# Expert slots in two phases and a router in batches of 4, 8 and 4 tiles, on one core of a Trainium2

## The chip, the cores and the metric

One core of one Trainium2 chip runs the whole program. The metric is the device time of one execution in microseconds (us), the median of three runs. Its engines work in parallel, each through its own queue in order: TensorE (PE; its weight loads are shown as PEld), VectorE (DVE), ScalarE (ACT), GpSimd (POOL) and SyncE (SP), which only starts transfers. Semaphores tie them together.

## The reference, cut to what matters

```python
x = x + linear_attention(cond_attention(x, ...), ...)     # x: (32, 64, 256), so 2048 tokens, 16 tiles of 128
# mixture of experts, 8 experts, hidden 128, top 2
logits = (x @ wt.T + repeat(cond @ wg.T)) / 2
topk_w, topk_idx = top_k(softmax(logits), 2);  topk_w = topk_w / (topk_w.sum(-1) + 1e-20)
y_e = (leaky(x @ w_gate[e]) * (x @ w_up[e])) @ w_down[e]  # for each token's two experts e
p = (leaky(x @ sw_gate) * (x @ sw_up)) @ sw_down          # shared experts, hidden 256, for all tokens
y = sum_k topk_w[k] * y_e[k] + p
x = x + relu(y @ W1 + b1) @ W2 + b2                       # dense layer, inner width 1024
```

All large products are made of three passes of split operands (an upper and a lower half, `_h` and `_l`), so each operand is written twice: a ScalarE copy for the upper half and a VectorE subtraction for the lower.

## The kernel before

Tokens lie in `xs`, 16 tiles (NT) of 128 rows. Attention runs as a software pipeline, `pipeline(e, body, after)`: step i works on tile i + 1 in the projection, i in the scores, i - 1 in the values, i - 2 and i - 3 in the second attention, up to step 18 (`LAST_I`). Tables such as `before_retrieving`, `while_retrieving`, `after_z`, `after_av`, `before_sums`, `before_uT` put further work into given steps by hand; each engine has its own tables. `xs` of tile i - 3 is final at the end of step i.

Routing works on batches of tiles (`BATCHES`, four of four tiles). Per batch: `x_transpose(g)` turns four tiles on TensorE, `x_upper` and `x_lower` split them, `logits(g)` multiplies them by the router's weights; VectorE takes the softmax and the top two (`router_logits`, `router_top`), `ranks(b)` counts on TensorE how many tokens stand ahead of each one for its expert, carried from batch to batch, and `router_places(b)` writes `posi`, the row of each token in a DRAM buffer `slot_x` with an area for each expert. GpSimd then scatters the tiles there, two indirect transfers per tile (L621).

The routed experts work on slots of 128 rows, each of one expert; 40 slots (SLOTS) hold any routing, worked on in 20 pairs. `slot_table` (L1176 on) computes from the counts which expert each slot has (`tab_w`, read into registers by TensorE), `slot_rows` from which row it is loaded (`tab_row`, read by SP). Per pair s and in this order in TensorE's loop: `slot_transpose(s + 1)` of the loaded rows `xq` (four buffers of pairs, XQ), `slot_gate_up(s)`, `slot_h_transpose(s - 1)`, `slot_down_project(s - 2)`. ScalarE and VectorE split the turned rows (`slot_x`, `slot_xl`), make the hidden layer (`slot_leak`, `slot_hidden`), split it (`slot_h`, `slot_hl`), and ScalarE copies the result out (`slot_y`). SP's queue, in order, loads pair s + 4 (`load_slots`, L404 on, two register loads and two transfers; it waits until the buffer is free) and stores pair s - 2 (`store_slots`, L412 on, which waits for `slot_y`). It starts after `tab` is 2 and all 32 scatters have landed (L416, L417). In the same loops stand `row_shift` and `row_table` (from where each token's results are gathered later), `second_bias` and `split_dense` (splitting of the dense layer's weights).

The shared experts are eight units n (four groups of tiles, two halves): `gate(n)`, `up(n)`, `down(n)` on TensorE; `unit_gate`, `unit_leak`, `unit_product`, `unit_upper`, `unit_lower` on ScalarE and VectorE; `shared_out` copies the sum. Four of them (EARLY) stand between attention and the slots, four behind the slots. Then GpSimd gathers the results (L629) and the dense layer runs.

```python
            e.wait_ge(sems['tab'], 2)
            e.wait_ge(sems['st_x'], 16 * 2 * NT)
            for s in range(XQ):
                load_slots(s)
```

## Time and profile before

| | |
|---|---|
| median of three runs | 503.66 us (502.45 to 508.02) |
| span of the profiled execution | 511.9 us |
| TensorE busy | 464.7 us, 91% |
| VectorE, ScalarE, GpSimd busy | 344.6, 260.3, 274.7 us |
| mean granted clock of TensorE | 0.938 of full |

The profiled execution is one run with the hardware profiler on, and its times start at its first instruction. Busy is the time in which an engine works; a clock of 1.00 is TensorE's 2.4 GHz, 0.50 is 1.2 GHz. Attention ends near 277 us, the slots are worked on from 322 to 383 us, the dense layer follows from about 410. A line number is that of the kernel, that of a helper where a helper issues the instruction.

### The profile page before, as it was taken

The numbers are of one execution on the slowest core, as the hardware profiler recorded it, in microseconds if no ns is written. First come the engines' busy times: TensorE is split into PE (matmuls) and PEld (weight loads), VectorE is DVE, ScalarE is ACT, GpSimd is POOL, SyncE is SP. The second block draws the span as 40 slices with busy tenths as digits, with TensorE's granted clock in tenths as the row PEclk, the third lists the DMA queues.
The fourth block names the chain that finished last, engine by engine and source line by source line (L and its number), as shares of the span: only waits on it lengthen the run. The fifth ranks groups of instructions, "written<-read, shape, count | busy, mean of one in ns | idle before, by whom it ended". The sixth has DMA issues, their size and how long they took to land.

```text
span 511.9 us, 11736 instructions
## 1 busy us (share of the span) xinstructions
PE 464.7 (91%) x4033; PEld 411.6 (80%) x4033; DVE 344.6 (67%) x873; ACT 260.3 (51%) x516; POOL 274.7 (54%) x299
## 2 busy tenths in 40 slices
PE   7796888999999999999997866599899999999996
PEld 4685787889888888888886756599897779898986
DVE  5787898888888888887763476287674635453522
ACT  4664465667675666665532013176664344444442
POOL 5789888897989797979356165000000551606000
PEclk9888999999999999999887595599999999999999
DMA  8651009073654610100022022545742210303001
GB/s 260 135 171 33 1 15 342 28 255 125 209 170 161 218 31 0 31 1 21 13 91 86 20 83 82 187 155 166 249 141 96 83 53 30 104 20 115 28 25 41
DMA packets 51663, 52.17 MB, mean 102 GB/s; under 512 B 6692, under 2 KB 49062, under 8 KB 51624
## 3 DMA queue, kind: packets, MB, share of 16 engines
q1 hardware_dynamic: 48004, 42.98, 26.6%
q0 software_dynamic: 3072, 8.39, 5.1%
q8 instruction: 23, 0.38, 0.3%
q10 hardware_dynamic: 548, 0.28, 0.2%
q14 instruction: 16, 0.13, 0.1%
HBM read 22.03 MB, written 29.62 MB: 101 GB/s over the span
## 4 chain that ended last, share of the span: by engine, by line
PE 55%; DVE 14%; POOL 12%; issue 9%; ACT 4%; DMA 2%; another core or an unknown queue 2%; SPq 1%; POOLq 0%; DVEq 0%; ACTq 0%
PE bank L332 8%; PE bank L333 7%; PE bank L334 7%; PE bank L337 5%; PE bank L338 5%; PE bank L1749 3%; POOL rn L605 2%; POOL sim L600 2%; PE bank L1518 2%; PE bank L1483 2%; PE bank L1453 2%; ACT oT_h L758 2%; POOL pr L585 2%; DVE oT_l L1075 2%
## 5 line engine op out<-in xcount | busy, mean ns | idle before, releaser
L629 POOL DMA_INDIRECT yg<-slot_y,yrow x32 | 34.4, 1074 | 122.5 <-DMA slot_y<-yb 78.7
L605 POOL TENSOR_TENSOR rn<-sc,half 128x6 f32<-128x6 f32 (+1 forms) x48 | 60.2, 1275 | 2.9 <-DVE sc L1064 1.8
L1318 DVE TENSOR_TENSOR hl<-hw,hh 128x512 fp32r<-128x512 f32 x32 | 22.2, 692 | 55.8 <-ACT hw L884 55.8
L621 POOL DMA_INDIRECT slot_x<-xs,posi x32 | 31.7, 989 | 34.7 <-DVE posi L1166 26.3
L882 ACT ACTIVATE hh<-bank,late 128x512 fp32r<-128x512 f32 x32 | 22.0, 688 | 52.2 <-PE bank L1749 42.0
L585 POOL TENSOR_TENSOR pr<-pe,rden 128x1024 f32<-128x1024 f32 x16 | 30.5, 1904 | 12.9 <-DVE rden L1092 12.1
L337 PE MATMUL bank<-wout_h,oT_h 128*128 128x256 f32 x128 | 32.5, 293 | 5.0 <-DVE oT_l L1075 5.0
L332 PE MATMUL bank<-wqkv_h,xnT_h 128*128 128x384 f32 x96 | 35.7, 372 | 1.2 <-DVE wqkv_l L912 0.6
L600 POOL TENSOR_TENSOR sim<-sim,mx 128x1040 f32<-128x1040 f32 x16 | 30.9, 1932 | 9.9 <-DVE mx L1053 9.9
L568 POOL TENSOR_TENSOR biasm<-bias,mneg 128x1040 f32<-128x1040 f32 x16 | 35.7, 2232 | 0.5 <-DMA bias<-rel_scratch 0.5
L1061 DVE TENSOR_REDUCE ss<-sq 128x6 f32<-128x384 f32 (+1 forms) x48 | 25.3, 527 | 12.3 <-ACT sq L744 12.3
L333 PE MATMUL bank<-wqkv_l,xnT_h 128*128 128x384 f32 x96 | 32.8, 341 | 0.0
L334 PE MATMUL bank<-wqkv_h,xnT_l 128*128 128x384 f32 x96 | 32.7, 341 | 0.0
L744 ACT ACTIVATE sq<-bank 128x384 f32<-128x384 f32 (+1 forms) x48 | 22.9, 477 | 19.0 <-PE bank L334 18.8
L337 PE MATMUL bank<-w_h,hh 128*128 128x256 f32 x128 | 32.5, 287 | 0.0
L338 PE MATMUL bank<-w_l,hh 128*128 128x256 f32 x128 | 32.0, 283 | 0.0
L1075 DVE SCALAR_TENSOR_TENSOR oT_l<-bank,colsc,oT_h 128x512 fp32r<-128x512 f32 x32 | 22.6, 746 | 13.0 <-ACT oT_h L758 12.9
L338 PE MATMUL bank<-wout_l,oT_h 128*128 128x256 f32 x128 | 31.0, 281 | 0.0
L722 ACT ACTIVATE zn<-bank,nb,rs 128x256 f32<-128x256 f32 x16 | 9.0, 564 | 41.9 <-POOL nb L594 37.3
L337 PEld LDWEIGHTS bank<-wout_h,oT_h 128*128 128x128 f32 x128 | 24.1, 188 | 7.6 <-DVE oT_l L1075 3.3
L332 PE MATMUL bank<-wu_h,bxT_h 128*128 x80 | 25.3, 316 | 2.5 <-DVE bxT_l L1257 2.5
L337 PEld LDWEIGHTS bank<-w_h,hh 128*128 128x128 f32 x128 | 24.3, 190 | 2.3 <-issue 1.4
(315 smaller groups left out, 1574.4 us busy)
## 6 DMA issues: line engine op xcount, KB each, us to landing
slot_x<-zrow SPq DMA_DIRECT2D x4, 4352.0 KB, 14.4
xq<-slot_x SPq DMA_DIRECT2D x40, 128.0 KB, 2.1
slot_y<-yb SPq DMA_DIRECT2D x20, 256.0 KB, 2.4
fstage<-in_f_W SPq DMA_DIRECT2D x4, 512.0 KB, 5.0
out<-p_all SPq DMA_DIRECT2D x8, 256.0 KB
raw_out<-in_c_Wout SPq DMA_DIRECT2D x2, 512.0 KB, 8.0
xs<-in_x SPq DMA_DIRECT2D x1, 1024.0 KB, 8.3
stage<-in_m_wgate SPq DMA_DIRECT2D x8, 128.0 KB
```

Source lines behind the costliest of these rows:

```text
L332: e.matmul(dst, stat[0], mov[0], start=start, stop=False, **kw)
L333: e.matmul(dst, stat[0], mov[1], start=False, stop=False, **kw)
L334: return e.matmul(dst, stat[1], mov[0], start=False, stop=stop, **kw)
L337: e.matmul(dst, stationary, moving[0], start=start, stop=False, **kw)
L338: e.matmul(dst, stationary, moving[1], start=False, stop=False, **kw)
L568: e.tensor_tensor(biasm[:, :, :], bias[:, :, :], (mneg[:, i:i + 1, :] if isinstance(i, int) else mneg[:, bass.ds(i, 1), :]).to_broadcast([ ...
L585: e.tensor_tensor(pr[:, :].rearrange('p (h k) -> p h k', h=H), pe[:, :, 0:S], rden[:, :].rearrange('p (h o) -> p h o', o=1).to_broadcast([ ...
L600: e.tensor_tensor(sim[:, :, :], sim[:, :, :], mx[:, :].rearrange('p (h o) -> p h o', o=1).to_broadcast([P, H, NK]), ALU.subtract).then_inc ...
L605: e.tensor_tensor(rn[:, lo:hi], sc[:, lo:hi], half[:, lo:hi], ALU.pow).then_inc(sems['rn'], 1)
L621: e.indirect_dma_start(out=xdram.ap()[:, :], out_offset=bass.IndirectOffsetOnAxis(ap=posi[:, t, r:r + 1], axis=0), in_=xs[:, t, :], in_off ...
L629: e.indirect_dma_start(out=yg[:, g % 2, r, t, :], out_offset=None, in_=ydram.ap()[:, :], in_offset=bass.IndirectOffsetOnAxis(ap=yrow[:, g ...
L1075: e.scalar_tensor_tensor(oT_l[:, :, b * S:(b + 1) * S], bank[6 + b][:, :].rearrange('p (c t) -> p c t', c=HP), col(NVC), oT_h[:, :, b * S: ...
```

## The change

Routing is cut into three batches of 4, 8 and 4 tiles. The slots are cut into two phases. Phase 0 has 16 slots (FULL), filled by the first twelve token tiles alone: these give 3072 routed rows, of which at least 16 whole slots of one expert can be made for any routing. Only slots that are full are taken. Phase 1 has the 24 other slots and everything that is left. So there are two tables (`slot_table(phase)`, `slot_rows(phase)`), two sets of counts, and `row_shift` has seven instructions in place of three. SP waits for the scatters of the first twelve tiles before phase 0 and for the other eight scatters (`st_xl`) before phase 1.

In the last attention steps, `x_transpose(1)` and `(2)`, `logits(2)` and `ranks(1)` come earlier, and unit 0 and the gate and up halves of unit 1 are put inside. The second phase's tables are computed inside phase 0's loop, the routing weights (before: sixteen small instructions ahead of the slots, now four) in phase 1's loop. Banks of PSUM are handed out anew. The split rows of each tile group get their own tensors (`xg0` to `xg3`).

```diff
-BATCHES = ((0, 4), (4, 4), (8, 4), (12, 4))
+BATCHES = ((0, 4), (4, 8), (12, 4))
 NB = len(BATCHES)
 CAP = T
 SLOTS = 2 * T // P + E
 WORD = 8
 PAIRS2 = SLOTS // 2
+FULL = 16
+FULL_PAIRS = FULL // 2
+PHASES = ((0, FULL), (FULL, SLOTS))
...
-            return bank[5 - n % 2] if n < EARLY else bank[n % 2 * 4]
+            return bank[(2, 2, 6, 4)[n]] if n < EARLY else bank[n % 2 * 4]
 
         def up_bank(n):
-            return bank[6 + n % 2] if n < EARLY else bank[1 + n % 2 * 4]
+            return bank[(3, 3, 7, 5)[n]] if n < EARLY else bank[1 + n % 2 * 4]
+
+        def rows_bank(g, k):
+            return bank[2 + k] if g < G - 1 else bank[4 + k]
+
+        def turned_bank(s):
+            return bank[s % 2 * 2]
+
+        def hidden_bank(s):
+            return bank[3 + s % 2]
+
+        def hidden_turned(s):
+            return bank[5][:, s % 2 * 2 * P:(s % 2 + 1) * 2 * P]
...
             e.wait_ge(sems['tab'], 2)
-            e.wait_ge(sems['st_x'], 16 * 2 * NT)
+            e.wait_ge(sems['st_x'], 16 * 2 * BATCHES[-1][0])
             for s in range(XQ):
                 load_slots(s)
             e.wait_ge(sems['unit'], due(U))
             for c in range(KD):
                 e.dma_start(fstage[:, c, :], kp('f_W1')[:, c, :]).then_inc(sems['ld_f'], 16)
-            for s in range(PAIRS2 + 2):
-                if s + XQ < PAIRS2:
+
+            def load_second(c):
+                e.wait_ge(sems['f_l'], due(c + 1))
+                e.dma_start(fstage[:, c, :].rearrange('p (k n) -> p k n', n=D), kp('f_W2')[:, c * 4:c * 4 + 4, :]).then_inc(sems['ld_f'], 16)
+            for s in range(FULL_PAIRS):
+                if s + XQ < FULL_PAIRS:
                     load_slots(s + XQ)
                 if s >= 2:
                     store_slots(s - 2)
-                if s == 9:
-                    for c in range(2):
-                        e.wait_ge(sems['f_l'], due(c + 1))
-                        e.dma_start(fstage[:, c, :].rearrange('p (k n) -> p k n', n=D), kp('f_W2')[:, c * 4:c * 4 + 4, :]).then_inc(sems['ld_f'], 16)
+            e.wait_ge(sems['tab'], 4)
+            e.wait_ge(sems['st_xl'], 16 * 2 * BATCHES[-1][1])
+            load_slots(FULL_PAIRS)
+            load_slots(FULL_PAIRS + 1)
+            store_slots(FULL_PAIRS - 2)
+            load_slots(FULL_PAIRS + 2)
+            load_slots(FULL_PAIRS + 3)
+            store_slots(FULL_PAIRS - 1)
+            for s in range(FULL_PAIRS, PAIRS2):
+                if s + XQ < PAIRS2:
+                    load_slots(s + XQ)
+                if s == FULL_PAIRS + 2:
+                    load_second(0)
+                    load_second(1)
+                if s >= FULL_PAIRS + 2:
+                    store_slots(s - 2)
+            store_slots(PAIRS2 - 2)
+            store_slots(PAIRS2 - 1)
...
-            after_xn = {-1: after_first_xn}
+            after_xn = {-1: after_first_xn, NT: lambda: x_upper(1)}
...
-            before_squares = {-1: before_first_squares, 0: decay_power, 1: wvo_upper, NT: lambda: x_upper(1)}
+            before_squares = {-1: before_first_squares, 0: decay_power, 1: wvo_upper, NT - 1: lambda: first_x()}
...
-            before_weights = {NT: lambda: router_exp(0)}
-            before_uT = {NT + 1: lambda: [router_exp(1), x_upper(2)]}
-
-            pipeline(e, body, {-1: lambda: wout_upper(1), 2: wt_upper, NT - 1: first_x})
-            e.wait_ge(sems['x1'], due(NT))
+            before_weights = {NT: lambda: router_exp(0), NT + 1: lambda: router_exp(1)}
+            before_uT = {NT: lambda: x_upper(2), NT + 1: lambda: unit_gate(0), LAST_I: lambda: [unit_upper(0), unit_gate(1)]}
...
-            after_xn = {-1: after_first_xn}
+            after_xn = {-1: after_first_xn, LAST_I: lambda: [unit_leak(0), unit_product(0)]}
...
-            before_retrieval = {0: lambda: row_stats(2), 3: decay_ready}
+            before_retrieval = {0: lambda: row_stats(2), 3: decay_ready, NT: lambda: x_lower(1)}
...
-            before_sums = {-1: before_first_sums, 3: lambda: [wvo_lower(), wt_lower()], NT: lambda: [router_top(0), x_lower(1)], NT + 1: lambda: router_top(1), LAST_I: lambda: x_lower(2)}
+            before_sums = {-1: before_first_sums, 3: lambda: [wvo_lower(), wt_lower()], NT - 1: lambda: x_lower(0), NT: lambda: router_top(0), NT + 1: lambda: router_top(1)}
...
-            before_norms = {0: fold_keys}
+            before_norms = {0: fold_keys, NT: lambda: x_lower(2)}
...
+            def slot_table(phase):
+                lo, hi = PHASES[phase]
+                n = hi - lo
+                e.wait_ge(sems['rank_t'], NB - 1 + phase)
+                counts = counts_at(phase).rearrange('p (e o) -> p e o', o=1).to_broadcast([P, E, 16])
+                edges = iota_j[:, 1 - phase:17 - phase].rearrange('p (o k) -> p o k', o=1).to_broadcast([P, E, 16])
+                rlink(e.scalar_tensor_tensor(nt_gt[:, :, :], edges, float(P), counts, ALU.mult, (ALU.is_le, ALU.is_lt)[phase]))
+                rlink(e.reduce_sum(avail[:, :], nt_gt[:, :, :], AX_X))
+                if phase == 1:
+                    rlink(e.tensor_tensor(avail[:, :], avail[:, :], own[:, 0, :], ALU.subtract))
+                rlink(e.tensor_tensor_scan(ends[:, phase, 1:E + 1], avail[:, :], limit[:, phase, :], 0.0, ALU.add, ALU.min))
+                rlink(e.tensor_tensor(ended[:, 0:n, :], iota_j[0:1, 0:n].rearrange('p (j o) -> p j o', o=1).to_broadcast([1, n, E - 1]), over_slots(ends[0:1, phase, 1:E], n), ALU.is_ge))
+                rlink(e.reduce_sum(slot_e[:, 0:n], ended[:, 0:n, :], AX_X))
+                rlink(e.tensor_tensor(slot_d[:, 0:n], slot_e[:, 0:n], powers[:, 0:n], ALU.mult))
+                words = slice(lo // WORD, hi // WORD)
+                rlink(e.reduce_sum(slot_w[:, words], slot_d[:, 0:n].rearrange('p (w n) -> p w n', n=WORD), AX_X))
+                e.tensor_copy(tab_w[0:1, words], slot_w[:, words]).then_inc(sems['tab'], 1)
+
+            def slot_rows(phase):
+                lo, hi = PHASES[phase]
+                n = hi - lo
+                rlink(e.tensor_tensor(own[:, phase, :], ends[:, phase, 1:E + 1], ends[:, phase, 0:E], ALU.subtract))
+                rlink(e.tensor_scalar(skip[:, :], own[:, phase, :], -1.0, float(CAP // P), ALU.mult, ALU.add))
+                if phase == 1:
+                    rlink(e.tensor_tensor(skip[:, 0:E - 1], skip[:, 0:E - 1], own[:, 0, 1:E], ALU.add))
+                    rlink(e.tensor_tensor(skip[:, 0:E - 1], skip[:, 0:E - 1], own[:, 0, 0:E - 1], ALU.subtract))
+                rlink(e.tensor_tensor(begun[:, 0:n, :], ended[:, 0:n, :], over_slots(skip[0:1, 0:E - 1], n), ALU.mult))
+                rlink(e.reduce_sum(slot_s[:, 0:n], begun[:, 0:n, :], AX_X))
+                if phase == 1:
+                    rlink(e.tensor_scalar(slot_s[:, 0:n], slot_s[:, 0:n], own[0:1, 0, 0:1], None, ALU.add))
+                rlink(e.tensor_tensor(slot_p[:, 0:n], slot_s[:, 0:n], iota_j[0:1, 0:n], ALU.add))
+                e.tensor_scalar(tab_row[0:1, lo:hi], slot_p[:, 0:n], float(P), None, ALU.mult).then_inc(sems['tab'], 1)
...
-            unit_leak(0)
+            pipeline(e, body, {-2: after_first_stats})
+            slot_table(0)
+            unit_lower(0)
+            unit_leak(1)
             x_lower(3)
+            unit_product(1)
+            split_unit(U - 1)
+            slot_rows(0)
             router_logits(2)
-            router_top(2)
-            unit_product(0)
-            router_places(2)
-            router_logits(3)
-            unit_lower(0)
-            router_top(3)
-            unit_leak(1)
-            unit_product(1)
-            for b in range(NB):
-                router_weights(b)
-            router_places(3)
-            split_unit(U - 1)
             unit_lower(1)
             unit_leak(2)
+            router_top(2)
             unit_product(2)
             unit_lower(2)
-            slot_table()
+            router_places(2)
             unit_leak(3)
             unit_product(3)
             unit_lower(3)
-            slot_rows()
+
...
             slot_xl(0)
-            for s in range(PAIRS2):
-                if s + 1 < PAIRS2:
+            for s in range(FULL_PAIRS):
+                if s + 1 < FULL_PAIRS:
                     slot_xl(s + 1)
                 slot_hidden(s)
                 if s >= 1:
                     slot_hl(s - 1)
-                if s == 2:
+                if s == 0:
+                    slot_table(1)
+                elif s == 1:
+                    slot_rows(1)
+                if s in (4, 6):
+                    split_dense((4, 6).index(s))
+            slot_xl(FULL_PAIRS)
+            slot_hl(FULL_PAIRS - 1)
+            for s in range(FULL_PAIRS, PAIRS2):
+                if s + 1 < PAIRS2:
+                    slot_xl(s + 1)
+                slot_hidden(s)
+                if s > FULL_PAIRS:
+                    slot_hl(s - 1)
+                if s == 9:
                     row_shift()
-                elif s == 3:
+                elif s == 10:
                     row_table()
-                elif s == 8:
+                elif s == 11:
+                    router_weights()
+                elif s == 12:
                     second_bias()
-                if s in (4, 6, 12, 14):
-                    split_dense((4, 6, 12, 14).index(s))
+                if s in (13, 15):
+                    split_dense(2 + (13, 15).index(s))
             slot_hl(PAIRS2 - 1)
...
-            before_retrieving = {NT: lambda: logits(0), NT + 1: lambda: logits(1), LAST_I: lambda: ranks(1)}
-            while_retrieving = {NT: lambda: x_transpose(1), LAST_I: first_gate}
+            before_retrieving = {NT: lambda: logits(0), NT + 1: lambda: logits(1), LAST_I: lambda: gate(1)}
+            while_retrieving = {NT + 1: lambda: [logits(2), first_gate()], LAST_I: lambda: [ranks(1), up(1)]}
...
-            after_z = {NT + 1: lambda: x_transpose(2)}
-            after_av = {NT: lambda: ranks(0)}
-            pipeline(e, body, {-1: after_first_projection, 0: after_first_scores, 1: after_second_scores})
+            after_z = {NT + 1: lambda: up(0)}
+            after_av = {NT: lambda: [x_transpose(2), ranks(0)]}
+            pipeline(e, body, {-1: after_first_projection, 0: after_first_scores, 1: after_second_scores, NT - 1: lambda: x_transpose(1)})
             e.wait_ge(sems['x1'], due(NT))
             x_transpose(3)
-            logits(2)
-            up(0)
+            gate(2)
             logits(3)
-            gate(1)
-            ranks(2)
-            up(1)
-            gate(2)
             up(2)
             down(0)
-            ranks(3)
+            down(1)
             gate(3)
+            ranks(2)
             up(3)
-            down(1)
             down(2)
             down(3)
-            e.wait_ge(sems['tab'], 1)
-            words = [e.value_load(tab_w[0:1, w:w + 1], min_val=0, max_val=E ** WORD - 1) for w in range(SLOTS // WORD)]
+            words = []
+
+            def load_words(phase):
+                e.wait_ge(sems['tab'], 2 * phase + 1)
+                for w in range(PHASES[phase][0] // WORD, PHASES[phase][1] // WORD):
+                    words.append(e.value_load(tab_w[0:1, w:w + 1], min_val=0, max_val=E ** WORD - 1))
+            load_words(0)
...
-                e.wait_ge(sems['bhl'], due(s - 1))
+                e.wait_ge(sems['bhl'], due(s))
...
-            e.wait_ge(sems['pos'], due(NB))
+            e.wait_ge(sems['unit'], U)
+            slot_transpose(0)
             e.wait_ge(sems['hw'], EARLY)
             e.wait_ge(sems['p'], 2 * (EARLY // NS))
-            e.wait_ge(sems['unit'], U)
-            slot_transpose(0)
-            for s in range(PAIRS2):
-                if s + 1 < PAIRS2:
+            for s in range(FULL_PAIRS):
+                if s + 1 < FULL_PAIRS:
                     slot_transpose(s + 1)
                 slot_gate_up(s)
                 if s >= 1:
                     slot_h_transpose(s - 1)
                 if s >= 2:
+                    slot_down_project(s - 2)
+            load_words(1)
+            slot_transpose(FULL_PAIRS)
+            slot_h_transpose(FULL_PAIRS - 1)
+            slot_down_project(FULL_PAIRS - 2)
+            for s in range(FULL_PAIRS, PAIRS2):
+                if s + 1 < PAIRS2:
+                    slot_transpose(s + 1)
+                slot_gate_up(s)
+                if s == FULL_PAIRS:
+                    slot_down_project(FULL_PAIRS - 1)
+                if s > FULL_PAIRS:
+                    slot_h_transpose(s - 1)
+                if s >= FULL_PAIRS + 2:
                     slot_down_project(s - 2)
             e.wait_ge(sems['bxl'], due(PAIRS2))
```

## Rows read from the trace of the kernel before

**Rows 1.** Busy time by stretches: length, PE, PEld, DVE, ACT, POOL, clock, DMA, GB/s.
```profile
250.00:268.10 18.10, 17.54 (x120) 15.95 (x119) 13.17 (x69) 8.07 (x18) 6.76 (x7) 0.81 0.18 59
268.10:281.00 12.90, 9.49 (x51) 8.10 (x50) 5.18 (x13) 3.18 (x6) 7.98 (x9) 0.74 0.24 83
...
319.00:327.20 8.20, 1.89 (x9) 1.51 (x9) 0.69 (x1) 1.30 (x3) 0.00 (x0) 0.70 0.36 100
327.20:333.50 6.30, 6.30 (x35) 6.30 (x34) 2.23 (x4) 1.93 (x5) 0.00 (x0) 0.58 0.79 268
```

**Rows 2.** Waits of 262 to 330 us: waiter, releaser, us, times, longest.
```profile
PE bank L1649 <- DMA xq<-slot_x: 7.0, 2, 4.2
```

**Rows 3.** Timeline of TensorE, slot transposes: start us, us, what, idle before.
```profile
322.46 1.09 PE L1649 MATMUL bank<-ident,xq 128*128 128x128 f32 x4 [4.16 <-DMA xq<-slot_x]
326.40 1.11 PE L1649 MATMUL bank<-ident,xq 128*128 128x128 f32 x4 [2.86 <-DMA xq<-slot_x]
...
333.18 0.60 PE L1649 MATMUL bank<-ident,xq 128*128 128x128 f32 x4
...
359.85 0.60 PE L1649 MATMUL bank<-ident,xq 128*128 128x128 f32 x4
...
362.63 0.60 PE L1649 MATMUL bank<-ident,xq 128*128 128x128 f32 x4
```

**Rows 4.** Timeline of SP's queue: loads of `xq`, a store, the next load.
```profile
319.10 8.56 SPq L410 DMA_DIRECT2D xq<-slot_x  x8
...
339.58 0.38 SPq L414 DMA_DIRECT2D slot_y<-yb  x1
340.72 1.42 SPq L410 DMA_DIRECT2D xq<-slot_x  x2
```

**Rows 5.** Chain that ended last, its piece before the slots.
```profile
315.64 2.39 DMA slot_x<-xs,posi
```

**Rows 6.** Timeline of GpSimd, batch 1: first and last of its eight scatters.
```profile
273.12 0.96 POOL L621 DMA_INDIRECT slot_x<-xs,posi  x1 [2.59 <-DVE posi L1166]
...
281.99 0.96 POOL L621 DMA_INDIRECT slot_x<-xs,posi  x1 [0.30 <-issue]
```

**Rows 7.** Timeline of VectorE: router of batch 1, late waits, slot table.
```profile
263.06 0.22 DVE L1130 TENSOR_REDUCE lg<-bank 128x32 f32<-128x64 f32 x1
...
267.51 0.24 DVE L1156 TENSOR_TENSOR_SCAN cs<-rmask,ohs 128x40 fp32r<-128x40 f32 x1
...
271.70 0.29 DVE L1044 SCALAR_TENSOR_TENSOR at<-bank,decay 128x128 f32<-128x128 f32 x1 [3.48 <-remote]
...
272.67 0.17 DVE L1166 CAST posi<-posf 128x8 uint32<-128x8 f32 x1
...
284.38 0.23 DVE L1130 TENSOR_REDUCE lg<-bank 128x32 f32<-128x64 f32 x1 [4.02 <-remote]
...
305.08 0.19 DVE L1163 SCALAR_TENSOR_TENSOR rk<-iota_e,bank 128x32 f32<-128x32 f32 x1 [2.51 <-remote]
...
310.12 0.28 DVE L1180 SCALAR_TENSOR_TENSOR nt_gt<-iota_j,bank 128x128 f32<-128x128 f32 x1
...
312.43 0.33 DVE L1187 CAST tab_w<-slot_w 1x5 int32<-1x5 f32 x1
```

**Rows 8.** Timeline of TensorE: first product of `logits(1)`, and the retrieval after it.
```profile
260.64 0.43 PE L1549 MATMUL bank<-cg,pair_of 2*128 2x64 f32 x2
...
262.81 0.69 PE L1467 MATMUL bank<-at,zn 128*128 128x128 f32 x4
```

**Rows 9.** Timeline of TensorE: first product of `up(1)`, `gate(2)` and `up(2)`.
```profile
292.20 0.77 PE L332 MATMUL bank<-x1A_h,wu_h 128*128 128x512 f32 x1
...
294.91 0.43 PE L332 MATMUL bank<-x1A_h,wu_h 128*128 128x512 f32 x1
...
296.33 0.40 PE L332 MATMUL bank<-x1A_h,wu_h 128*128 128x512 f32 x1
```

**Rows 10.** Timeline of ScalarE: `slot_y` of one pair.
```profile
362.83 0.60 ACT L845 ACTIVATE yb<-bank 128x512 f32<-128x512 f32 x1 [0.27 <-PE bank L334]
```

More of the change, by code:

```diff
@@ L216, in adaln_attention_ffn @@
         p_all = sb('p_all', [P, NT, D])
+        rest = sb('rest', [P, 72])
         gs = sb('gs', [P, GT])
@@ L505, in slot_constants @@
                     e.wait_ge(sems['pc'], upto('pc'))
-                    last = e.memset(rmask[b][:, :, 0:1], 0.0)
+                    e.memset(rmask[b][:, :, 0:1], 0.0)
+                e.memset(ends[:, :, 0:1], 0.0)
+                for n, (lo, hi) in enumerate(PHASES):
+                    last = e.memset(limit[:, n, :], float(hi - lo))
                 last.then_inc(sems['p_const'], 1)
@@ L1196, in row_shift, with router_weights @@
[L1196 to L1199 removed]
+            def router_weights():
+                rlink(e.reduce_sum(tsum[:, :], top[:, :, 0:2], AX_X))
+                rlink(e.tensor_scalar(tsum[:, :], tsum[:, :], 1e-20, None, ALU.add))
+                rlink(e.reciprocal(trec[:, :], tsum[:, :]))
+                rlink(e.tensor_tensor(topw[:, :, :], top[:, :, 0:2], trec[:, :].rearrange('p (t o) -> p t o', o=1).to_broadcast([P, NT, 2]), ALU.mult))
@@ L1588, in down @@
                 e.wait_ge(sems['p'], due(2 * g))
[L1589 removed]
+                e.wait_ge(sems['hw'], 2)
                 for t in range(TG):
@@ L1687, in _ @@
                 if s >= 2:
+                    slot_down_project(s - 2)
[3 more added lines that the diff above has]
+            slot_down_project(FULL_PAIRS - 2)
+            for s in range(FULL_PAIRS, PAIRS2):
+                if s + 1 < PAIRS2:
+                    slot_transpose(s + 1)
+                slot_gate_up(s)
+                if s == FULL_PAIRS:
+                    slot_down_project(FULL_PAIRS - 1)
+                if s > FULL_PAIRS:
+                    slot_h_transpose(s - 1)
+                if s >= FULL_PAIRS + 2:
                     slot_down_project(s - 2)
```

181 lines of the change are left out of this document (93 added, 88 removed).

## The prediction

> **What bounds the kernel now.** I read the 40 slices of the page first: TensorE is busy for nine tenths or more nearly everywhere, except from about 268 to 333 us, where its share and its granted clock both fall. The busy time by stretches shows the same hole in numbers [rows 1]: 9.5 of 12.9 us busy at 268 to 281 with a mean clock of 0.74 of full, 1.9 of 8.2 us at 319 to 327, and 0.58 of full clock in the 6.3 us after it. That hole lies between the end of attention and the first expert slots. The waits of 262 to 330 us name its last link: TensorE waited 7.0 us for `xq`, the tokens gathered per expert [rows 2].
>
> Then I followed that link backwards. The first transposes of a slot pair start at 322.46, after 4.16 us of waiting [rows 3]. `xq` is loaded by SP from 319.10 on [rows 4], after the last scatter into `slot_x`, started at 315.64, has landed 2.39 us later [rows 5]. The scatters are issued by GpSimd, eight for each batch of four token tiles, from 273.12 to 281.99 in seven steps, so 1.27 us each [rows 6]. Each batch starts when VectorE has written `posi` (272.67 plus 0.17 for batch 1, [rows 7]). So today the first slot waits for four batches, and the last batch's places are begun at 305.08 only. Expert work can't begin before the last token is scattered. The change attacks that.
>
> **How the profiled time stands to the median.** The span is 511.9 us, the median of the three timed runs 503.66, 8.2 less. I make the sum on the trace and carry the difference to the median, with one correction below.
>
> **The earlier start (the gain).** The first 16 slots now need token tiles 0 to 11 alone. What sets them is `posi` of the new batch 1 (tiles 4 to 11); call its time T.
> TensorE: `x_transpose(1)` moves in front of step 16 (eight transposes; four take 0.60 us in [rows 3]) and `x_transpose(2)` into step 16, so step 17 runs about 1 us later. Its `logits(1)` lay at 260.64 to 262.81, 2.2 us [rows 8]. With the shift and the retrieval matmuls after it, `logits(2)`, also 2.2, ends at 261.64 + 2.2 + 0.7 + 2.2 = 266.7. VectorE then took 4.7 us for four tiles from the first reduction at 263.06 to the end of the scan at 267.75 [rows 7]; eight tiles add four maxima and four index searches, about 1 us: 272.4. Meanwhile TensorE has `gate(0)` and `up(0)` (1.4 each at full clock, 2.7 at half: 294.91 to 296.33 against 292.20 to 294.91, [rows 9]) and the old rest of the step, and after them come the score product, `unit_leak(0)` and `unit_product(0)` on VectorE, `gate(1)`, the retrieval and `ranks(1)`, then 1.2 us for the places (four small instructions, the slot table's eight took 2.6, [rows 7]). `at`, the score tile, is queued on VectorE behind leak and product, and `ranks(1)` on TensorE behind `gate(1)` and behind that `at`. At full clock I get T = 276.7, at half clock 280; I take 277.5, nearer the full clock, since TensorE was busy for 17.5 of the 18.1 us of steps 16 and 17 and still had 0.81 [rows 1], and the gap behind them is now filled with unit work.
> From T: 0.3 to the first scatter, 15 x 1.27 = 19.05 to the sixteenth, 2.39 to land, 1.07 to SP's first load, and 322.46 - 319.10 = 3.36 to the transposes: T + 26.2 = 303.7. Against 322.46 that is 18.8 us earlier.
> The shared units must be done as well. In the new order I count their chain (VectorE holds `slot_table(0)`, `x_lower(3)`, `router_top(2)` and four leak/product/lower groups between them) to 299 at full and 305 at half clock. So they hide under the scatters, or cost 1.3 at worst. The last batch's eight scatters follow on GpSimd to about 308 and land 20 us before they are needed: nothing.
>
> **The hand-over between the phases (the main loss).** Before, pair s + 4 is loaded while pair s is worked on, and a pair takes 362.63 - 359.85 = 2.78 us [rows 3]. Now SP's `load_slots(8)` is queued behind `store_slots(5)`, which waits for ScalarE's `slot_y(5)`, which waits for the down product of pair 5, the last thing that TensorE has in phase 0. On SP's queue behind that store stand loads 8 and 9, then `store_slots(6)`, loads 10 and 11. From the end of that product: 0.27 + 0.60 for `yb` [rows 10], 0.4 for the store, 0.75 to read the row register (from the end of a store at 339.96 to the next load at 340.72, [rows 4]), then the 3.36 of above: 5.4 us in which TensorE has nothing, since `slot_transpose(8)` stands in front of the work left over. Pair 9 lands 2.1 later, while 1.3 of work is there: 0.8. Load 10 waits for `store_slots(6)`, so for the down product of pair 6, and lands 6.6 after pair 8, while work lasts to 4.7: 1.9. Later SP needs about 2.7 for a pair's two loads and store (2 x 1.07 from the eight loads in 8.56 us, 0.38, a start), as much as TensorE, so the lead doesn't come back, but nothing more is lost than 0.5. Sum 8.1 + 0.5. Bounds: 5.4 if pairs 9 and 10 come in time, 12 if the first load is a straggler, as pair 1 was (326.40 for a load issued 2.1 after pair 0's, [rows 3]).
> **Clock.** After today's gap of this kind the 6.3 us from 327.2 ran at 0.58 of full clock [rows 1]; two early pairs, without their down product, took 3.4 us each (326.40 to 333.18, [rows 3]); at full clock such a pair would take 2.0. I take 2.5 for the hand-over, between 0 and 8.
> By the Trainium skill ("TensorE: Matmul & The Clock Gate", "HAM oscillation — how this bites in real kernels") a wait for a transfer between bursts makes the next burst start at the low clock; the row agrees, and taken to its end it is the third rival.
> **VectorE inside the loops.** `slot_table` took 2.6 us (310.12 to 312.76, eight instructions, [rows 7]). The second table and rows, nine and nine instructions on fewer elements, cost about 2.2 and 2.0, in iterations 0 and 1 of phase 0, in front of `slot_xl(2)` and `slot_xl(3)`, for which `slot_gate_up` waits. An iteration leaves VectorE about 1 us. 4.2 less what slack covers: 2.5, between 0 and 4.2. The seven instructions of `row_shift`, the table, the weights (four, were sixteen, now off the path ahead of the slots) and the bias follow in pairs 9 to 12: 0.7. The new banks cost a wait of `slot_h_transpose` for `bhl` one pair earlier; the down product right behind it needed it already: 0.
>
> **The correction.** Three of VectorE's waits in the old hole have no visible releaser: for `at` until 271.70, for the logits until 284.38, for the ranks until 305.08 [rows 7]. VectorE sat idle 3.48, 4.02 and 2.51 us ahead of them, 10.0 together, and each is a product of TensorE asked for while scatters are being issued. Some of that is plain waiting; I count half, 5.0, as lateness. If it belongs to the profiled execution alone, the old start in the timed runs is up to 5.0 us earlier than in the trace, and the gain that much smaller. The new order puts the same work beside the same scatters. Between 0 and 5.0 I take 1.5, nearer to 0 since nothing in the trace says that the timed runs lack it.
>
> **Sum:** -18.8 + 8.1 + 0.5 + 2.5 + 2.5 + 0.7 + 1.5 = -3.0. Profiled 508.9, median 503.66 - 3.0 = **500.7 us**. Everything behind the slots (units 4 to 7 and the dense layer) is not touched.
>
> **Rivals.**
> *Small gain, mostly handed back* (as above): 500.7, of itself 496 to 505. Chance 0.45.
> *The hand-over is paid, the rest is hidden*: the tables fit in the wait for the second pair, which was 3.9 us long [rows 3], the clock stays up, the lateness is real in timed runs: -18.8 + 8.1 + 0.5 + 0.7 = -9.5, 494. For it: VectorE stood idle there. Against it: the 0.58 after the old gap. Chance 0.20.
> *Slower by the clock*: the two gaps of the hand-over come close together, and TensorE goes on at half clock in the pairs behind them. A pair at half clock costs about 2 more (3.4 against 2.0 without the down product, and 0.6 for that). Five pairs beyond the 2.5 counted: -3.0 + 10 = +7, 510.7. It decides from four pairs on (+5). For it: 0.74 at 268 to 281 although the engine was three quarters busy. Against it: full clock came back within 6 us of dense work at 333. Chance 0.17.
> *The slots don't start so early*: the lateness of TensorE's results falls on `ranks(1)`, now the one product that all waits for; T is 282 or later. -3.0 + 4.5 = +1.5, 505. Chance 0.18.
>
> **Chances.** A measurement of this kernel can tell about 1% from no change (498.6 and 508.7 are the edges). Faster: the second rival's 0.20 and a third of the forecast's, 0.15: 0.35. Slower: the clock's 0.17. Same: 0.48. The range runs from just under the second case to above the fourth, 493 to 508.
>
> **What would show it.** `posi` of the second batch at 276 to 280; the first `xq` transposes at 302 to 306; a TensorE wait for `xq` of about 5 us between the seventh and ninth pair and one of about 2 us two pairs later, a granted clock of half after it; small waits of `slot_gate_up` for `bxT_l` in the first three pairs; the stretch behind the slots as long as before. Wrong would be: no gap at the hand-over (then SP's order isn't what I take it for), or a first slot after 308.

## The result

The changed kernel takes 511.81 us (median of four runs, 510.61 to 515.11), the kernel before beside it 503.55 us. The ratio is 1.016, with a 95% interval of 1.010 to 1.022: slower by 1.6%, where 500.7 us and a range up to 508 had been forecast. With both kernels measured side by side on another chip the ratio was 1.012 [1.006, 1.018].

The span of its profiled execution is 508.9 us, the very number that the prediction has for it. Part of that is luck. Against the trace that the sum was made on, pair 0 starts 16.25 us earlier (forecast 18.8) and everything behind costs 13.25 (forecast 14.3). The 1.5 that closes the gap is the correction, which by the prediction's own words belongs to the timed runs and not to the span.

And that trace was not like the runs that the median is made of. Here the span plus 1.7 us is the time of the same run (508.9 and 510.61). By that the profiled execution of the kernel before, with its span of 511.9, stands for a run of about 513.6 us (an estimate) and not of 503.66.

Busy time of the changed kernel by stretches (length, PE, PEld, DVE, ACT, POOL, clock, DMA, GB/s), to be set beside [rows 1]:

```profile
268.10:281.00 12.90, 11.80 (x60) 9.56 (x61) 9.03 (x50) 3.64 (x8) 4.51 (x5) 0.89 0.15 52
...
295.00:305.00 10.00, 4.32 (x30) 3.68 (x28) 3.16 (x8) 2.19 (x5) 7.83 (x8) 1.00 0.34 119
305.00:319.00 14.00, 9.29 (x59) 8.50 (x60) 6.94 (x23) 3.71 (x8) 3.95 (x5) 0.76 0.68 227
...
333.50:383.40 49.90, 38.61 (x295) 37.03 (x294) 29.66 (x68) 23.67 (x52) 0.00 (x0) 0.93 0.48 149
```

The hole at 319 to 327 is gone, since the slots start earlier; TensorE's wait for them now lies at 295 to 305, with 4.3 of 10 us busy. A new hole is in the last row: TensorE is busy for 38.6 of 49.9 us. The timeline of TensorE, transposes of slot pairs 0, 1, 7, 8, 9, 10, 11 and 19, shows both, to be set beside [rows 3]:

```profile
306.21 1.09 PE L1742 MATMUL bank<-ident,xq 128*128 128x128 f32 x4 [5.47 <-DMA xq<-slot_x]
309.09 1.08 PE L1742 MATMUL bank<-ident,xq 128*128 128x128 f32 x4 [1.79 <-DMA xq<-slot_x]
...
328.76 0.60 PE L1742 MATMUL bank<-ident,xq 128*128 128x128 f32 x4
339.90 1.12 PE L1742 MATMUL bank<-ident,xq 128*128 128x128 f32 x4 [5.03 <-DMA xq<-slot_x]
342.52 0.71 PE L1742 MATMUL bank<-ident,xq 128*128 128x128 f32 x4
347.72 0.66 PE L1742 MATMUL bank<-ident,xq 128*128 128x128 f32 x4 [2.37 <-DMA xq<-slot_x]
350.18 0.66 PE L1742 MATMUL bank<-ident,xq 128*128 128x128 f32 x4
...
378.90 0.60 PE L1742 MATMUL bank<-ident,xq 128*128 128x128 f32 x4
```

Pair 0 starts at 306.21, 16.25 us before the 322.46 of [rows 3]. Pair 8, the first of the second phase, comes 11.1 us after pair 7. SP's queue in that place, to be set beside [rows 4]:

```profile
326.80 9.09 SPq L438 DMA_DIRECT2D slot_y<-yb  x4
336.72 3.65 SPq L434 DMA_DIRECT2D xq<-slot_x  x4
343.38 0.38 SPq L438 DMA_DIRECT2D slot_y<-yb  x1
344.53 3.96 SPq L434 DMA_DIRECT2D xq<-slot_x  x4
```

Four stores in a row, then four loads: the loads of pairs 8 and 9 stand behind the store of pair 5.

### The profile page after: what moved, and what is told of

It is laid out like the page before. It is cut to its first block, busy times and chain, and to the rows that moved or that the text cites. A ratio compares the mean times of both kernels' runs of the same rounds, so it can differ in the third digit from the quotient of the medians.

```text
span 508.9 us, 11728 instructions
## 1 busy us (share of the span) xinstructions
PE 457.9 (90%) x4032; PEld 404.9 (80%) x4032; DVE 342.9 (67%) x867; ACT 260.4 (51%) x515; POOL 275.1 (54%) x300
## 3 DMA queue, kind: packets, MB, share of 16 engines
q0 software_dynamic: 3072, 8.39, 5.2%
## 4 chain that ended last, share of the span: by engine, by line
PE 55%; POOL 15%; DVE 11%; issue 8%; ACT 4%; DMA 3%; SPq 2%; POOLq 0%; DVEq 0%; ACTq 0%
PE bank L356 8%; PE bank L358 7%; PE bank L357 7%; PE bank L361 5%; PE bank L362 5%; POOL slot_x L666 3%; PE bank L1855 3%; POOL sim L645 3%; POOL rn L650 3%; POOL pr L630 2%; PE bank L1606 2%; DVE den L1144 2%; POOL wu_l L617 2%; ACT oT_h L803 2%; PE bank L1571 2%
## 5 line engine op out<-in xcount | busy, mean ns | idle before, releaser
L630 POOL TENSOR_TENSOR pr<-pe,rden 128x1024 f32<-128x1024 f32 x16 | 30.4, 1903 | 13.1 <-DVE rden L1147 12.3
L1116 DVE TENSOR_REDUCE ss<-sq 128x6 f32<-128x384 f32 (+1 forms) x48 | 25.3, 527 | 12.3 <-ACT sq L789 12.3
L789 ACT ACTIVATE sq<-bank 128x384 f32<-128x384 f32 (+1 forms) x48 | 23.0, 478 | 18.9 <-PE bank L358 18.8
L1329 DVE TENSOR_TENSOR bxT_l<-bank,bxT_h 128x512 fp32r<-128x512 f32 x20 | 13.7, 686 | 25.7 <-ACT bxT_h L870 25.6
```

Source lines behind the costliest of these rows:

```text
L630: e.tensor_tensor(pr[:, :].rearrange('p (h k) -> p h k', h=H), pe[:, :, 0:S], rden[:, :].rearrange('p (h o) -> p h o', o=1).to_broadcast([ ...
L1116: e.reduce_sum(ss[:, lo:hi], sq[:, lo:hi, :], AX_X).then_inc(sems['ss'], 1)
```

## The experiments

Twelve runs follow, on three chips; some repeat a kernel. Each ratio is to the kernel before beside it on the same chip, with its 95% interval. On the first chip the kernel before took 502.6 us, on the other two 510.9 and 511.3; times of different chips are not compared.

**The kernel before, again** (unchanged).

> The kernel before, unchanged, profiled again. Theory one: the profiled execution of before was an unusual one, its three late waits of VectorE (3.48, 4.02, 2.51 us) are not in ordinary executions. Then this trace has a span near 502, no such waits, and the first slot transposes at about 312 to 314 instead of 322.5. Rival: those waits belong to the kernel, and the kernel after is slower for another reason. Then the hole is as before, first slot at 322, span near 512.

502.50 us, 1.001 [0.998, 1.004], span 501.0. VectorE's timeline at the three instructions that waited late in [rows 7]:

```profile
268.33 0.29 DVE L1044 SCALAR_TENSOR_TENSOR at<-bank,decay 128x128 f32<-128x128 f32 x1 [0.77 <-PE bank L1447]
...
275.36 0.23 DVE L1130 TENSOR_REDUCE lg<-bank 128x32 f32<-128x64 f32 x1 [0.76 <-PE bank L1555]
...
294.84 0.19 DVE L1163 SCALAR_TENSOR_TENSOR rk<-iota_e,bank 128x32 f32<-128x32 f32 x1
```

The waits were 3.48, 4.02 and 2.51 us with no visible releaser; here they are 0.77, 0.76 and none. The third instruction comes 10.2 us earlier (294.84 against 305.08), and the slots with it. Its transposes of pairs 0, 7, 11 and 19:

```profile
312.26 1.08 PE L1649 MATMUL bank<-ident,xq 128*128 128x128 f32 x4 [4.21 <-DMA xq<-slot_x]
...
332.70 0.60 PE L1649 MATMUL bank<-ident,xq 128*128 128x128 f32 x4
...
345.42 0.60 PE L1649 MATMUL bank<-ident,xq 128*128 128x128 f32 x4
...
370.59 0.60 PE L1649 MATMUL bank<-ident,xq 128*128 128x128 f32 x4
```

With this trace the 7.9 us between the spans (508.9 - 501.0) fall into parts: the start 306.21 - 312.26 = -6.05; pairs 0 to 7, 22.55 against 20.44, +2.1; pairs 7 to 11, 21.42 against 12.72, +8.7; pairs 11 to 19, 28.72 against 25.17, +3.5; behind them -0.4.

Each of these is a difference of two single traces. The changed kernel and the three versions of it that follow on this chip have pair 0 at 305.74 to 309.36, so the gain of 6.05 at the start is uncertain by some 3 us.

**Loads inside the loop.** The changed kernel, but SP loads pair s + 4 in pair s across the border too.

```diff
-            for s in range(FULL_PAIRS):
-                if s + XQ < FULL_PAIRS:
-                    load_slots(s + XQ)
...
+            for s in range(PAIRS2 + 2):
+                if s + XQ == FULL_PAIRS:
+                    e.wait_ge(sems['tab'], 4)
+                    e.wait_ge(sems['st_xl'], 16 * 2 * BATCHES[-1][1])
```

> The kernel after, with one edit on SP's queue: pair 8 and those behind it are loaded four pairs ahead, as all others are, and the wait for the last batch's scatters stands ahead of load 8 in iteration 4. Theory (the hand-over is the loss): pairs 7 to 11 take 12.7 us instead of 21.5, and SP's lead stays, so 8 to 11 us less than after, 500 to 503. Rival (the pace of SP's queue or of the transfers bounds the slots anyway): not more than 3 us less.

501.88 us, 0.997 [0.994, 1.001]. Its pairs 7, 8, 11 and 19:

```profile
330.37 0.60 PE L1730 MATMUL bank<-ident,xq 128*128 128x128 f32 x4
338.05 0.63 PE L1730 MATMUL bank<-ident,xq 128*128 128x128 f32 x4 [1.52 <-issue]
...
344.62 0.60 PE L1730 MATMUL bank<-ident,xq 128*128 128x128 f32 x4
...
369.94 0.60 PE L1730 MATMUL bank<-ident,xq 128*128 128x128 f32 x4
```

Pairs 7 to 11 take 14.25 in place of 21.42, pairs 11 to 19 25.32 in place of 28.72: SP's order cost 7.2 and 3.4 us, 10.6 together. From pair 0 to the end, with small losses elsewhere, 9.8 are won (192.9 in place of 202.7). The rival, at most 3, falls. What is left at the border is a wait of 1.52 without a transfer, in front of the second table's words, which TensorE reads into registers there (`load_words(1)`).

**Tables early.** The changed kernel, but the second table and rows are made ahead of the loop.

```diff
+            slot_table(1)
+            slot_rows(1)
             slot_xl(0)
```

> The kernel after, with the second phase's table and rows computed by VectorE ahead of the first pair, while it waits for the gathered tokens, instead of inside iterations 0 and 1. Theory: it removes the stalls of pairs 2 to 4, 1 to 2.5 us less than after. Rival: these stalls are hidden or made up for at the hand-over, which waits for pair 5's result and is reached that much earlier: then still 1 to 2 us less; if the hand-over is bound by something absolute in time, 0.

508.22 us, 1.014 [1.010, 1.018]. Pairs 0 to 7 take 20.43 (305.74 to 326.17) in place of 22.55, just what the kernel before needs; pairs 7 to 11 take 21.89, so the border stays. The tables cost 2.1. The spans differ by 2.6 (508.9 and 506.3).

**Both.**

> The kernel after with both edits. Theory: the two add up, 9 to 13 us less than after, 498 to 502, some us below the kernel before. Rival: as soon as the hand-over is gone SP's queue is the bound and the tables' time is hidden by it: the same as with the loads alone.

499.18 us, 0.996 [0.992, 1.000]. Pairs 7 to 11: 14.16. By the ratios alone this could as well be the kernel with the loads (0.997), since the intervals overlap, and the two spans are equal (500.1 and 500.2). But in this execution even the places of the first batch, which no edit touches, came 3.2 us later than in the changed kernel's trace (262.98 against 259.73), and pair 0 at 309.36. Counted from pair 0 to the end, the changed kernel takes 202.7 us, the loads save 9.8, the tables 2.1, and both 11.9. The two edits add up, and the rival falls.

**One loop.** Both, and every engine runs one loop of 20 pairs again; the second table's words are read before pair 0.

```diff
+            load_words(1)
             slot_transpose(0)
-            for s in range(FULL_PAIRS):
+            for s in range(PAIRS2):
```

> The changed kernel with one loop of 20 slot pairs again on every engine, as before the change, the loads of pair s + 4 inside it, the second slot table made before the first pair's tokens are split, and the seven register loads' partner on TensorE (the second table's words) moved in front of the first pair. Only the order of the slots and the routing batches of the change are left. My theory (the early start is worth about 6 us against an ordinary execution of the kernel before, and the hand-over gives it back): from the eighth to the twelfth pair TensorE needs the 12.7 us that it needs in the kernel before, against 21.5 in the changed kernel; the first transposes lie at 306 to 310, the span is 497 to 499, the time 499 to 501, so 0.991 to 0.997 of before. The rival (the two phases themselves, not their hand-over, cost the time, by the clock): pairs 7 to 11 still take 16 or more, and the time stays at 503 to 508.

503.68 us, 0.991 [0.988, 0.994]; pairs 7 to 11 take 12.86 (335.26 to 348.12), the kernel before's 12.7. The rival (16 or more) falls, though the time lies in its range: the chip is a slower one, and only the ratio can be set beside the forecast. TensorE's wait of about 1.5 us without a releaser, at the border in the two kernels with the loads inside (1.52 and 1.46), now stands before pair 0 (1.48), where `load_words(1)` went. But the start was late, at 311.62, and pair 1's at 317.08, after 4.37 us of waiting for `p_all`, a shared unit's result. Again, on the third chip:

> The one-loop kernel again, on the same chip as the kernel before and the changed kernel. In its first run the first transposes came at 315.9 us, behind waits without a visible releaser, and it still took 0.991 of before. My theory: without such waits the first transposes lie at 306 to 310 and the span is 495 to 499, about 12 below the changed kernel's; with them it is as in the first run, 503. Against the changed kernel it is 8 to 13 us faster in either case (the hand-over).

504.36 us, 0.988 [0.983, 0.994]. (The 315.9 in the expectation is the start of ScalarE's copy to `p_all`; the first transposes of that run came at 311.62.) It is faster than the kernel before beside it. It is 0.976 of the changed kernel beside it (504.36 / 516.67), 12.3 us. Both edits in two loops stood at 0.996 where the changed kernel had 1.016, so 0.980 of it; with intervals of half a per cent on each ratio nothing here shows that one loop is better, and it never ran on the first chip. My 495 to 499 for a trace without late results wasn't tested: here they were present again (ScalarE waited 13.4 us for a unit's result, with no visible releaser).

**One loop that waits for all scatters.** The start alone.

```diff
+            e.wait_ge(sems['st_xl'], 16 * 2 * BATCHES[-1][1])
             for s in range(XQ):
                 load_slots(s)
```

> The same kernel with one wait more: SP loads no slot of the first sixteen before the last batch of four token tiles is scattered too. It measures what the early start is worth by itself. My theory: the first transposes come eight scatters of 1.27 us later, so about 10 us, at 316 to 319, and the time is 8 to 10 us longer than with the early start (508 to 511). The rival (the pairs that start early run slower, since the scatters and the shared units are still in their way): the start is 10 us later, but the time only 3 to 6 longer.

511.90 us, 1.007 [1.002, 1.012]. Against the one-loop kernel the first transposes come 8.4 us later (320.05 against 311.62), and the median is 8.2 higher. By the medians the early start is worth 8 us. By the two profiled spans (508.0 and 503.4) it is 4.6, as the rival had it: the early pair 1 lost 4.37 us to a shared unit's result. So the rival is not excluded for an execution with such a wait.

**The changed kernel, waiting for all scatters.**

> The changed kernel with one wait more: SP loads no slot of the first phase before the last batch of four token tiles is scattered. Everything else, the hand-over too, is as in the changed kernel. If the change's parts add up, the time is the changed kernel's 511.8 plus the 8 to 10 us of eight scatters, 519 to 522: the hand-over is paid and nothing is won. If the hand-over's stall lies partly in tables and transfers that a later start gives more time, it is 515 to 518.

524.16 us, 1.033 [1.027, 1.040]; the changed kernel has 1.012 on the third chip, so about 2.1%, 11 us, a little more than my 8 to 10; the changed kernel did not run on this chip. The border costs the same when the start is late: 340.19 to 351.33 from pair 7 to 8, 5.01 of it waiting for `xq`.

**The kernel before, on the third chip.**

> The kernel before, unchanged, a third time, beside the changed kernel. The first repeat had a span of 501.0 us and none of the three waits of VectorE that have no visible releaser; the profiled execution that the prediction was made on had them, 10.0 us together, and a span of 511.9. In the runs beside the one-loop kernel the same kernel took 506 to 520, median 510.9. If such waits are a thing of the chip or of the hour that comes and goes with the kernel's own time, this trace shows them when its time is near 511, and none when it is near 503. If they are noise of one execution, they stand in no relation to the time.

510.94 us, 0.999 [0.995, 1.003], span 508.5. The same three instructions:

```profile
271.20 0.29 DVE L1044 SCALAR_TENSOR_TENSOR at<-bank,decay 128x128 f32<-128x128 f32 x1 [3.19 <-remote]
...
282.47 0.23 DVE L1130 TENSOR_REDUCE lg<-bank 128x32 f32<-128x64 f32 x1 [3.73 <-remote]
...
303.15 0.19 DVE L1163 SCALAR_TENSOR_TENSOR rk<-iota_e,bank 128x32 f32<-128x32 f32 x1 [2.50 <-remote]
```

3.19, 3.73 and 2.50, where [rows 7] have 3.48, 4.02 and 2.51: the late results are no noise of one execution. They come at the same three places, and with a time that is 8 us longer. They go with the chip, or with what is done on it at that hour. The four traces of the second chip have waits without a releaser in this region too, the four of the first chip none.

**The changed kernel, on the third chip.**

> The changed kernel, unchanged, on the same chip as the kernel before. By my theory (the 10 us of late results in the profiled execution hid a start gain of 6 us, and the hand-over takes 8.7 back) it is slower than before by 1 to 2% where the late results are absent, and near 0 to 1% where the kernel before shows them, since its own scatters pause for 7.5 us just there. The rival (the late results hit both alike): the ratio is 1.016 on either.

516.67 us, 1.012 [1.006, 1.018], span 515.8. I had expected it nearer to the kernel before; the interval holds the rival's 1.016 as well, and the spans speak for the rival (below). It has late results too, at other places: ScalarE's for two shared units, and through the second of them the second pair.

```profile
297.35 1.09 ACT L854 ACTIVATE p_all<-bank 128x512 f32<-128x512 f32 x2 [7.28 <-remote]
...
314.59 1.08 ACT L854 ACTIVATE p_all<-bank 128x512 f32<-128x512 f32 x2 [10.03 <-remote]
```

```profile
308.26 1.08 PE L1742 MATMUL bank<-ident,xq 128*128 128x128 f32 x4
315.77 1.09 PE L1742 MATMUL bank<-ident,xq 128*128 128x128 f32 x4 [6.43 <-ACT p_all L854]
```

The kernel before pays 7.5 us of span on this chip (508.5 - 501.0) and the changed one 6.9 (515.8 - 508.9): 2.05 at the start of pair 0 and 5.83 in pairs 0 to 7, where the late results are, less 1.0 behind. So the difference between the kernels is 7.3 here and 7.9 there: late results hit both nearly alike.

**Plain stores for the scatters.** The kernel before, but GpSimd stores the same rows at fixed places; the tokens are not sorted by expert, so it leaves out what the slots need and is no candidate.

```diff
-                        e.indirect_dma_start(out=xdram.ap()[:, :], ...
+                        e.dma_start(xdram.ap()[(2 * t + r) * P:(2 * t + r + 1) * P, :], xs[:, t, :])
```

> The kernel before with each of GpSimd's 32 indirect scatters into slot_x replaced by a plain DMA of the same 128 rows of 1 KB to fixed rows, on the same queue and behind the same waits; the tokens are thus not sorted by expert (the lookup of the expert slots' tokens is left out). My theory: the late results of TensorE come with GpSimd's indirect scatters, so no wait of VectorE without a releaser is left between 262 and 310 us, and the first slot, which then waits for the last batch's places and not for eight scatters of 1.27 us, starts 7 to 9 us earlier: 6 to 9 us less than before, and its times lie close together. The rival (the late results come from something else, the traffic or the chip): they remain, at the same places.

500.71 us, 0.977 [0.969, 0.985], span 500.2, on the chip where the kernel before showed the late results:

```profile
269.87 0.29 DVE L1044 SCALAR_TENSOR_TENSOR at<-bank,decay 128x128 f32<-128x128 f32 x1 [1.24 <-PE bank L1447]
...
276.93 0.22 DVE L1130 TENSOR_REDUCE lg<-bank 128x32 f32<-128x64 f32 x1 [0.76 <-PE bank L1555]
...
295.36 0.19 DVE L1163 SCALAR_TENSOR_TENSOR rk<-iota_e,bank 128x32 f32<-128x32 f32 x1
...
306.97 0.17 DVE L1194 TENSOR_SCALAR tab_row<-slot_p 1x40 int32<-1x40 f32 x1
```

No late wait is left, so here they went with the indirect transfers. What about those transfers matters isn't separated: the plain stores also keep GpSimd busy for less than half the time. One product in the prediction's trace points to the scatters too. The ranks of batch 2 were ready at 292.37 by the record and taken at 292.40, while no scatter was being issued between 282.95 and 293.63:

```profile
292.40 0.19 DVE L1163 SCALAR_TENSOR_TENSOR rk<-iota_e,bank 128x32 f32<-128x32 f32 x1 [3.40 <-PE bank L1565]
```

The second half of my expectation was wrong, though. A store took GpSimd 0.53 us (eight in 4.25) and not 1.27, yet the first slot starts at 311.60, only 0.7 earlier than the 312.26 of the undisturbed kernel before. There the row table, written at 306.97, sets the start, in VectorE's queue behind the shared units' work. Of the 9.0 us (320.61 to 311.60) 8.35 are what the kernel before itself lacks on the first chip; the pace of the scatters gave almost nothing.

**Four batches.** The one-loop kernel with four batches of four tiles, so that GpSimd isn't idle from 271.5 to 279.0.

```diff
-BATCHES = ((0, 4), (4, 8), (12, 4))
+BATCHES = ((0, 4), (4, 4), (8, 4), (12, 4))
```

> The one-loop kernel with the routing in four batches of four token tiles, as before the change, in place of batches of 4, 8 and 4. GpSimd, idle for 7.5 us in the changed kernel until the places of its batch of eight are known, can then go on with the scatters of tiles 4 to 7 as in the kernel before. My theory (GpSimd's 24 scatters of 1.27 us set the first slot): the first transposes come 5 to 7 us earlier than in the one-loop kernel, at about 300 to 303, and the time is 492 to 496, if the shared units are done by then (302 in the changed kernel). The rival (the shared units, or the ranks of the third batch, set the start): at most 2 us are won, 497 to 500.

507.93 us, 0.999 [0.995, 1.003]: 4.2 slower than the one-loop kernel beside it, against my theory, with the first transposes at 319.29 and not at 300 to 303. VectorE's wait for the last tile's attention product, and TensorE's timeline around it (the last product, the next work):

```profile
290.82 0.42 DVE L1114 TENSOR_TENSOR xs<-bank,xs 128x256 f32<-128x256 f32 x1 [7.89 <-remote]
```

```profile
283.68 0.28 PE L358 MATMUL bank<-wvo_h,rT_l 128*128 128x256 f32 x1
291.30 1.11 PE L1588 MATMUL bank<-ident,xs 128*128 128x128 f32 x4 [7.35 <-issue]
```

The product was over at 283.96 by its record, and VectorE took it at 290.82, while sixteen scatters ran without a break. Nothing else was under way on TensorE, VectorE or ScalarE. So this kernel is no test of what earlier scatters are worth where results are not late; that stays open.

## Why the prediction was wrong

**The step that failed is the correction.** The prediction saw the three late waits, 10.0 us, and the question that they raise: do the timed runs have them? It took 1.5 of 5.0. In the undisturbed trace the whole 10.2 us were missing: pair 0 starts at 312.26 and not at 322.46, and the gain is smaller by all of it. That the timed runs of the prediction were undisturbed too is inferred: their 503.55 lies beside the first chip's 502.6 and not beside 510.9 and 511.3, and the changed kernel's trace of that measurement has no such wait. The same error stands in "I carry the difference to the median": a span 8.2 above the median of its own kernel was taken for a constant, where a span is 1.7 below its own run's time. The two together, a span that is 10 too long and 10 us of unexplained waits, were the answer.

Had the late results been real everywhere, the forecast would still have failed: the new start was worked out from durations without them, and compared with a trace that has them. On the chip that shows them both kernels pay, 7.5 and 6.9, and the changed one is still slower, by 1.2%.

**The new start**: forecast 303.7, found 306.21. T was 278.7 (forecast 277.5); fifteen scatters took 20.1, not 19.05, one of them 1.72 long; SP and the transfer 0.2 and 0.1 more. 2.5 in all. The shared units hid under the scatters, as forecast. The undisturbed gain is so 6.05 in place of 18.8 - 1.5 = 17.3.

**The hand-over**: forecast 8.1 in the pairs around the border, 0.5 behind, 2.5 for the clock, 0.7 for the small work: 11.8. Found +8.7 and +3.5 = 12.2. The first wait was 5.03 (forecast 5.4), the third 2.37 (1.9); the second was hidden (0.8). The 0.5 for SP's lost lead was too little: a wait of 1.62 us for `xq` came at pair 15, and the loads in the loop brought 3.4 back behind the border. The split is seen in TensorE's busy time: pairs 7 to 11 and 11 to 19 of the undisturbed kernel before, then of the changed one.

```profile
332.70:345.42 12.72, 11.69 (x98) 11.22 (x97) 10.19 (x23) 7.81 (x17) 0.00 (x0) 1.00 0.59 182
345.42:370.59 25.17, 23.13 (x195) 22.46 (x194) 17.00 (x35) 15.53 (x34) 0.00 (x0) 1.00 0.63 200
```

```profile
328.76:350.18 21.42, 13.33 (x99) 12.46 (x97) 9.25 (x19) 8.31 (x18) 0.00 (x0) 0.92 0.34 108
350.18:378.90 28.72, 24.95 (x192) 24.02 (x193) 21.35 (x52) 15.61 (x35) 0.00 (x0) 0.94 0.57 178
```

About the same number of products took 1.6 and 1.8 us longer, at a clock of 0.92 and 0.94 in place of 1.00. So of the 12.2 us some 3.5 are the clock (forecast 2.5) and 8.8 are idle time (forecast 8.1 + 0.5, and the 0.7). With the loads ahead the clock was 1.00 in both stretches, and 25.3 us sufficed for pairs 11 to 19, the kernel before's 25.2. This part of the prediction was right in its mechanism, and its sum was 0.4 short.

**The tables**: forecast 2.5, found 2.1, by the trace and by taking them away.

**Behind the slots**: nothing forecast, -0.4 found.

So the losses were 14.3 by forecast and 13.95 by trace, and the gain 17.3 against 6.05: -3.0 + 11.25 - 0.35 = +7.9. The rival "slower by the clock" named nearly the right time, 510.7, but for a reason that hardly happened: it needed 12.5 us from the clock (its 10 and the 2.5), and the runs show 3.5. "The slots don't start so early" priced late results at 4.5 in the new order alone. None of the rivals had it that the old start was earlier than its trace. Nearly all signs that the prediction asked for came (`posi` at 278.73, the first `xq` at 306.21, waits of 5.03 and 2.37, 130.0 us behind the slots as before). They all look at the changed kernel, and the error lay in the other one.

TensorE's clock in the hand-over: behind the wait of 5.03 us it was 0.50 for 2.6 us of work, behind the wait of 2.37 it was 1.00 at once, and it fell to 0.50 once more at 366.8, after 4.3 us of which TensorE was busy for 1.8.

```profile
339.90:342.50 2.60, 2.60 (x12) 2.60 (x13) 0.82 (x2) 0.87 (x2) 0.00 (x0) 0.50 0.35 107
362.50:366.80 4.30, 1.78 (x13) 1.51 (x13) 1.92 (x5) 3.24 (x7) 0.00 (x0) 0.98 0.53 159
366.80:370.00 3.20, 3.20 (x17) 3.20 (x16) 2.78 (x5) 1.45 (x4) 0.00 (x0) 0.50 0.56 174
```

The prediction names the Trainium skill ("TensorE: Matmul & The Clock Gate", "HAM oscillation — how this bites in real kernels") for a burst that starts at the low clock behind a wait for a transfer. The trace agrees for the first wait (0.50) and not for the second (1.00).

## What to carry to other kernels

Compare a profiled execution's own time with the timed runs before summing on it; where its span is longer than their median, look for waits without a releaser, and make the sum with them and without them, on both sides of the comparison. When a loop is cut into phases, let the queue that loads ahead run across the border: here the order of one DMA queue took back 10.6 us in pairs 7 to 19, more than the early start gave. A store that waits for the end of the pipeline must not stand before a load that feeds its beginning. Ask for signs on both sides of the comparison, and not only in the changed kernel. And ask what else is ready just before the thing that is taken away: without the scatters' pace the row table set the start, 0.7 us earlier.

## What the runs showed of the hardware

While GpSimd issues indirect scatters, an engine that waits for a product of TensorE can take it long after the end of the product's record: 1.7, 3.3 and 5.5 us after it at the three places in the prediction's trace (VectorE was idle for 3.48, 4.02 and 2.51 us there), and 6.9 in the four-batch kernel (283.96 to 290.82). In the undisturbed trace it was 0.03 and 0.04 us at the first two places, with the same scatters under way.

All traces of the second and third chip in which scatters are issued show such waits, none of the first chip's does, and with plain stores of the same rows they were gone (one run). In the kernel before they fell on the same three instructions in both traces. In the one-loop kernel they did not: the first trace has 7.26 and 9.45 us of ScalarE for `p_all` and 1.95 of VectorE, the second 13.35 for `p_all`. Whether the product or its signal is late the records can't tell, since the ends of products are modelled in them, and why one chip has none of it stays open. The same kernel took 502.6 us on one chip and 511 on two others; between the traces of the first and the third, 8.35 us lie ahead of pair 0 (312.26 and 320.61).
